# Swapping the two 32-query blocks of the early half in an attention kernel, so that every row tile has five value products

## The reference, cut to what matters

```python
xn = layernorm(x, g_in)                       # x: (64, 128, 512)
q = (xn @ Wq).reshape(b, n, 16, 64).transpose(0, 2, 1, 3) * 64 ** -0.5
k, v = split(xn @ Wkv)                        # one k and one v head of 64, plus a null key and value
sim = einsum('bhid,bjd->bhij', q, k) + bias   # bias: (16, 128, 128), and a null column
sim = where(causal_mask, neg, sim)            # query i sees keys 0..i and the null key
sim = where(mask_p[:, None, None, :], sim, neg)
out = einsum('bhij,bjd->bhid', softmax(sim), v)
return x + layernorm(out.reshape(b, n, 1024) @ Wo, g_out)
```

## Time and profile before

| what | value |
|---|---|
| three timed runs | 1069.54, 1069.09, 1062.03 us (median 1069.09) |
| profiled execution, its own time | 1064.88 us |
| its span, from the first to the last instruction | 1063.0 us |
| mean granted TensorE clock | 0.989 of full speed |

### The profile page before, as it was taken

The page is one execution under the profiler, slowest core; times in us unless marked ns, Lnnn a source line. Parts: engine busy times, 40 slices in busy tenths (PEclk is TensorE's granted clock), DMA queues, the critical chain, the costliest instruction groups (busy, mean ns, idle before and its releaser), DMA issues.

```text
span 1063.0 us, 42980 instructions
## 1 busy us (share of the span) xinstructions
PE 1029.5 (97%) x14254; PEld 902.9 (85%) x14254; DVE 765.8 (72%) x3513; ACT 661.2 (62%) x2620; POOL 828.9 (78%) x1488
## 2 busy tenths in 40 slices
PE   6789999999999999999999999999999999999986
PEld 6678898888888888888888888888888889889875
DVE  4777777777777777786777787776777777777663
ACT  5655675666675665675665676565676565666552
POOL 2867887778878778878778788788788778787775
PEclk8999999999999999999999999999999999999998
DMA  7312222232222222222223122223222223121101
GB/s 213 124 34 86 77 81 89 67 94 76 63 85 82 74 87 73 68 84 85 76 82 91 50 87 84 86 70 89 62 78 85 83 73 93 54 84 59 50 25 60
DMA packets 90013, 84.01 MB, mean 79 GB/s; under 512 B 21568, under 2 KB 64064, under 8 KB 89792
## 3 DMA queue, kind: packets, MB, share of 16 engines
q1 hardware_dynamic: 88336, 81.03, 25.3%
q10 hardware_dynamic: 1456, 0.04, 0.1%
HBM read 40.11 MB, written 16.78 MB: 54 GB/s over the span
## 4 chain that ended last, share of the span: by engine, by line
PE 89%; issue 2%; POOL 2%; ACT 2%; DVE 1%; POOLq 0%; DVEq 0%; ACTq 0%
PE ps_proj L500 38%; PE ps_pv L488 33%; PE ps_s L452 9%; PE ps_pv L477 9%; ACT exp_bot L914 1%; POOL w_nrm L1112 1%; ACT exp_top L914 1%; POOL y_out L1156 0%; POOL y_nrm L1152 0%; DVE logit_bot L608 0%; DVE o_lo L630 0%; POOL bias_b L1103 0%; ACT xn L942 0%; POOL small L1138 0%; DVE wt L624 0%
## 5 line engine op out<-in xcount | busy, mean ns | idle before, releaser
L914 ACT ACTIVATE exp_bot<-logit_bot,neg_max 128x129 f32<-128x129 f32 x512 | 201.6, 399 | 252.0 <-DVE neg_max L608 223.0
L1103 POOL TENSOR_TENSOR bias_b<-bias_c,mask_add 128x256 f32<-128x256 f32 (+1 forms) x512 | 291.9, 599 | 45.3 <-DVE neg_max L608 45.2
L500 PE MATMUL ps_proj<-xt_hi,wq_hi 128*128 128x256 f32 x1024 | 302.5, 295 | 7.5 <-DVE q_sb L690 6.0
L500 PE MATMUL ps_proj<-xt_lo,wq_hi 128*128 128x256 f32 x1024 | 288.6, 282 | 0.9 <-issue 0.9
L500 PE MATMUL ps_proj<-xt_hi,wq_lo 128*128 128x256 f32 x1024 | 288.6, 282 | 0.0
L608 DVE CUSTOM_DVE_ANT_0 logit_bot<-ps_s,bias_b 128x128 f32<-128x128 f32 x512 | 128.3, 288 | 180.1 <-PE ps_s L452 162.4
L500 PEld LDWEIGHTS ps_proj<-xt_hi,wq_hi 128*128 128x128 f32 x1024 | 193.3, 189 | 24.9 <-issue 13.0
L1112 POOL TENSOR_TENSOR w_nrm<-exp_bot,w_inv 128x256 f32<-128x256 f32 x256 | 156.9, 613 | 65.2 <-DVE w_inv L617 65.2
L488 PE MATMUL ps_pv<-wo_hi,o_hi 128*128 128x512 f32 x488 | 199.0, 408 | 1.2 <-DVE o_lo L630 1.2
L488 PE MATMUL ps_pv<-wo_lo,o_hi 128*128 128x512 f32 x488 | 193.5, 397 | 0.0
L500 PEld LDWEIGHTS ps_proj<-xt_hi,wq_lo 128*128 128x128 f32 x1024 | 193.4, 189 | 0.0
(11 more groups left out here) (94 smaller groups left out, 1778.6 us busy)
## 6 DMA issues: line engine op xcount, KB each, us to landing
x_in<-in_x_dram SPq DMA_DIRECT2D x32, 512.0 KB, 4.1
x_res<-in_x_dram SPq DMA_DIRECT2D x64, 256.0 KB, 2.9
out_dram<-y_out SPq DMA_DIRECT2D x64, 256.0 KB, 2.1
x_split<-xn SPq DMA_DIRECT2D x480, 32.0 KB, 1.9
v_rep<-v_raw SPq DMA_DIRECT2D x256, 32.0 KB, 1.9
w_raw<-in_L_cond_Wq_dram SPq DMA_DIRECT2D x4, 512.0 KB, 11.7
w_raw<-in_L_cond_Wo_dram SPq DMA_DIRECT2D x4, 512.0 KB, 5.2
mask_u<-in_mask_BxS_bk_dram SPq DMA_DIRECT2D x31, 32.0 KB, 3.7
```

The costliest lines, as they stand in the source:

```text
L500: mm = pe.matmul(ps[:, 0:TOK], w[:, k, cols], xt[:, slot, k], start=(j == 0), stop=(j == len(todo) - 1))
L914: ins = nc.scalar.activation(out_[:, s, j], in_[:, s, j], ACT.Exp, bias=neg_max[:, s, k:k + 1], scale=-1.0, accum_out=w_sum[:, s, k:k + 1])
L1103: ins = nc.gpsimd.tensor_tensor(out_, bias, key_mask, ALU.add)
```

## The change

x's query and key blocks are put in the order 1, 0, 2, 3 within a batch (`PLACED`): the two 32-token blocks of the early half trade places. The row tile that has three late products then has two early ones (block 1, key blocks 0 and 1), and the one with four late products has one early (block 0). The products per row tile become 5, 5, 5, 5 in place of 4, 6, 4, 6; there are still 40 matmuls in the program per call. What goes with it:

- `split_x` writes to the swapped block, and PE's two early transposes become matmuls with `placing`, a permuted identity, made on DVE at the start.
- Stores and reloads of the residual are three DMAs (32, 32 and 64 rows) in place of one, `PIECES` = 3.
- The mask is added in swapped order by two DVE instructions in place of one.
- The bias is loaded by 12 DMAs into a spare buffer (`q_sb` of the second slot) and made head by head: five GpSimd instructions for each of four, and a `causal_early` mask of its own, built at the start. DVE waits for the bias before it first writes that slot of `q_sb`.

The core of the diff (the semaphore counts that follow from three pieces are left out):

```diff
+PLACED = (1, 0, 2, 3)
 ITEMS = (
-    [(1, 0), (1, 1), (1, 2), (0, 0)],
-    [(1, 0), (1, 1), (1, 2), (1, 3), (0, 0), (0, 1)],
+    [(1, 0), (1, 1), (1, 2), (0, 0), (0, 1)],
+    [(1, 0), (1, 1), (1, 2), (1, 3), (0, 1)],
 )
...
+        placing = sb("placing", [P, P])

...
-        COL_LOADS, ROW_LOADS, BIAS_LOADS, V_LOADS = 4, 2, 8, 8
+        COL_LOADS, ROW_LOADS, BIAS_LOADS, V_LOADS = 4, 2, 12, 8
+        bias_raw = q_sb[:, 1].rearrange("p c u n -> p (c u n)")[:, 0:CB * (BOT + TOP)].rearrange(
+            "p (c n) -> p c n", c=CB)
+        PIECES = 3
         SPLITS = (N // BLK) * (P // BLK)
...
             return o[:, g // 2].rearrange("p c (l h q) -> p c l h q", l=2, h=2)[:, :, :, g % 2]
+
+        def early_swapped(keys_):
+            return keys_.rearrange("p e (a j) -> p e a j", j=BLK)[:, :, 1::-1]
+
+        def placed(rows):
+            return ((rows[0:BLK], slice(BLK, HALF)), (rows[BLK:HALF], slice(0, BLK)), (rows[HALF:N], slice(HALF, N)))
...
             def load_res(q, i):
-                sp.dma_start(x_res[:, i % GB], x_pairs[q, :, i, :]).then_inc(ld_res[i % GB], 16)
+                for rows, at in placed(x_pairs[q, :, i, :]):
+                    sp.dma_start(x_res[at, i % GB], rows).then_inc(ld_res[i % GB], 16)
...
                     for r in range(P // BLK):
-                        sp.dma_start(x_split[BLK * r:BLK * (r + 1), :, a],
+                        sp.dma_start(x_split[BLK * r:BLK * (r + 1), :, PLACED[a]],
                                      xn[BLK * a:BLK * (a + 1), :, P * r:P * (r + 1)]).then_inc(ld_split, 16)
...
                 for e in range(2):
-                    sp.dma_start(bias_c[up, :, N * e:N * (e + 1)], by_head[u, e, HALF:N]).then_inc(ld_bias, 16)
-                    sp.dma_start(bias_c[up, :, BOT + HALF * e:BOT + HALF * (e + 1)],
-                                 by_head[u, e, 0:HALF, :, 0:HALF]).then_inc(ld_bias, 16)
+                    sp.dma_start(bias_raw[up, :, N * e:N * (e + 1)], by_head[u, e, HALF:N]).then_inc(ld_bias, 16)
+                    for a in range(2):
+                        row = HALF * u + BLK * PLACED[a]
+                        sp.dma_start(bias_raw[row:row + BLK, :, BOT + HALF * e:BOT + HALF * (e + 1)],
+                                     by_head[u, e, BLK * a:BLK * (a + 1), :, 0:HALF]).then_inc(ld_bias, 16)
             load_x(0, 1)
...
                         k, b = KX * i + j // GB, j % GB
-                        mm = pe.transpose(ps[:, N * j:N * (j + 1)], xn[:, b, P * k:P * (k + 1)], ident[:])
+                        mm = pe.matmul(ps[:, N * j:N * (j + 1)], xn[:, b, P * k:P * (k + 1)], placing[:],
+                                       start=(j == 0), stop=(j == KX * GB - 1))
                 elif kind == "kv":
...
                 pe.wait_ge(ident_made, 1)
+                pe.wait_ge(placing_made, 2)
                 for _ in range(WARM):
...
                 wait(dve, bias_b_made, CG * (f - 1))
-                nc.vector.tensor_scalar(mask_add[:, k], mask_u8[:, k], MASKED, -MASKED, ALU.mult,
-                                        ALU.add).then_inc(mask_made, 1)
+                nc.vector.tensor_scalar(mask_add[:, k, :, 0:HALF].rearrange("p b (a j) -> p b a j", j=BLK),
+                                        early_swapped(mask_u8[:, k, :, 0:HALF]), MASKED, -MASKED, ALU.mult, ALU.add)
+                nc.vector.tensor_scalar(mask_add[:, k, :, HALF:N], mask_u8[:, k, :, HALF:N], MASKED, -MASKED,
+                                        ALU.mult, ALU.add).then_inc(mask_made, 1)
...
             nc.vector.memset(logit_top[:, :, :, HALF:HALF + 1], 0.0).then_inc(filled, 1)
+            dve.wait_ge(ident_made, 1)
+            nc.vector.tensor_copy(placing[:].rearrange("p (a j) -> p a j", j=BLK)[:, 0:2],
+                                  ident[:].rearrange("p (a j) -> p a j", j=BLK)[:, 1::-1]).then_inc(placing_made, 1)
+            nc.vector.tensor_copy(placing[:, HALF:N], ident[:, HALF:N]).then_inc(placing_made, 1)
             x_stats_of(0, 0)
...
                 inverse(3, 3)
+                dve.wait_ge(bias_made, 3 * CB)
                 q_copies(1, 0)
...
             pool.wait_ge(causal_made, 2)
+            nc.gpsimd.memset(causal_early[:], 0.0).then_inc(early_zero, 1)
+            pool.wait_ge(early_zero, 1)
+            for u in range(2):
+                row = HALF * u + BLK
+                nc.gpsimd.memset(causal_early[row:row + BLK, 0:BLK], -MASKED).then_inc(early_filled, 1)
+            pool.wait_ge(early_filled, 2)
+            for g in range(P // BLK):
+                row, h = BLK * g, g % 2
+                own = causal_early[row:row + BLK, BLK * h:BLK * (h + 1)]
+                nc.gpsimd.affine_select(out=own, in_=own, compare_op=ALU.is_ge, fill=-MASKED, base=0,
+                                        pattern=[[-1, BLK]], channel_multiplier=1).then_inc(early_filled, 1)
+            pool.wait_ge(early_filled, 6)
             pool.wait_ge(filled, 1)
...
-            def make_bias(i):
-                cs = slice(2 * i, 2 * i + 2)
-                for k, part in enumerate((bias_c[:, cs, 0:BOT], bias_c[:, cs, BOT:])):
-                    part = part.rearrange("p c (e n) -> p c e n", e=2)
-                    shift = nb_row[:, cs].unsqueeze(3).to_broadcast(list(part.shape))
-                    nc.gpsimd.tensor_tensor(part, part, shift, ALU.subtract).then_inc(bias_shifted, 1)
-                pool.wait_ge(bias_shifted, 2 * i + 2)
-                for keys_, part in ((N, bias_c[:, cs, 0:BOT]), (HALF, bias_c[:, cs, BOT:])):
-                    own = part.rearrange("p c (e n) -> p c e n", e=2)[:, :, :, keys_ - HALF:keys_]
-                    mask_ = causal[:].unsqueeze(1).unsqueeze(1).to_broadcast(list(own.shape))
-                    nc.gpsimd.tensor_tensor(own, own, mask_, ALU.add).then_inc(bias_made, 1)
-                pool.wait_ge(bias_made, 2 * i + 2)
+            def make_bias(c):
+                null = nb_row[:, c].unsqueeze(2).to_broadcast([P, 2, HALF])
+                null_blocks = nb_row[:, c].unsqueeze(2).unsqueeze(3).to_broadcast([P, 2, 2, BLK])
+                raw_late, raw_early = bot_top(bias_raw[:, c])
+                late, early = bot_top(bias_c[:, c])
+                nc.gpsimd.tensor_tensor(late[:, :, 0:HALF].rearrange("p e (a j) -> p e a j", j=BLK),
+                                        early_swapped(raw_late[:, :, 0:HALF]), null_blocks,
+                                        ALU.subtract).then_inc(bias_made, 1)
+                nc.gpsimd.tensor_tensor(late[:, :, HALF:N], raw_late[:, :, HALF:N], null,
+                                        ALU.subtract).then_inc(bias_shifted, 1)
+                nc.gpsimd.tensor_tensor(early.rearrange("p e (a j) -> p e a j", j=BLK), early_swapped(raw_early),
+                                        null_blocks, ALU.subtract).then_inc(bias_shifted, 1)
+                pool.wait_ge(bias_shifted, 2 * c + 2)
+                for own, mask_ in ((late[:, :, HALF:N], causal), (early, causal_early)):
+                    nc.gpsimd.tensor_tensor(own, own, mask_[:].unsqueeze(1).to_broadcast([P, 2, HALF]),
+                                            ALU.add).then_inc(bias_made, 1)
+                pool.wait_ge(bias_made, 3 * c + 3)
...
                 make_bias(0)
+                make_bias(1)
                 bias(0)
                 bias(1)
-                make_bias(1)
+                make_bias(2)
+                make_bias(3)
                 x_rstd_of(1)
...
```

More of the change, by code:

```diff
@@ L105, in attention_block @@
         causal = sb("causal", [P, HALF])
+        causal_early = sb("causal_early", [P, HALF])
         eps_col = cols(2)
@@ L180, in attention_block @@
         causal_zero, causal_made = sem("causal_zero"), sem("causal_made")
+        early_zero = sem("early_zero")
+        placing_made, early_filled = sem("placing_made"), sem("early_filled")
         filled = sem("filled")
@@ L364, in store @@
                 apart(sp)
-                sp.dma_start(out_pairs[p + back // (2 * GB), :, back % (2 * GB), :], y_out[:, b]).then_inc(stored[b], 16)
+                for rows, at in placed(out_pairs[p + back // (2 * GB), :, back % (2 * GB), :]):
+                    sp.dma_start(rows, y_out[at, b]).then_inc(stored[b], 16)
                 if reload:
@@ L369, in _ @@
             for b in range(GB):
-                sp.sem_inc(stored[b], 16)
+                sp.sem_inc(stored[b], 16 * PIECES)
             load_x(0, 0)
@@ L432, in _ @@
             for b in range(GB):
-                sp.wait_ge(stored[b], 16 * GROUPS + 16)
+                sp.wait_ge(stored[b], 16 * PIECES * (GROUPS + 1))
         @block.tensor
@@ L895, in last_out @@
                 dve.wait_ge(y_rstd_made, B)
-                dve.wait_ge(ld_res[b], 16 * GROUPS)
-                dve.wait_ge(stored[b], 16 * GROUPS)
+                dve.wait_ge(ld_res[b], 16 * PIECES * GROUPS)
+                dve.wait_ge(stored[b], 16 * PIECES * GROUPS)
```

(6 more changed lines are left out.)

## The result

The changed kernel takes 1083.98 us (median of 4 runs, 1083.03 to 1085.23), the kernel before in the same session 1067.82 (4 runs). The ratio is 1.0162 with a 95% interval of 1.012 to 1.0204: slower by some 1.6%, clear of no change, and above the range of the prediction. The profiled execution has a span of 1083.4 us against 1063.0, so 20.4 us have to be found.

A forecast was written before the change was run, and what follows sets the result against it. The prediction took PE, busy without a gap from 110 to 1020 us, as the bound. Its terms, -12.7 + 3.3 + 0 + 0.7 = -8.7 us, gave a forecast of 1057.5 us, range 1049 to 1075.

The forecast's parts named there:

- the waves: PE's value calls: two of 12 matmul waves go, 0.205 us in each of 62 calls, 12.7 us gained.
- The rival that issue holds PE to 17 ns a start: Value calls: issue of the 80 matmuls sets the pace, no waves saved, +4.0 us, 1070 us; chance 0.10.
- the start: Before the loop: longer bias work on GpSimd, later bias DMAs and doubled transposes cost 3.3 us, bounds 1.8 and 7.0.
- what PE saves in this stretch is saved whole: From 110 to 1020 us PE is busy for 908.76 of 910 us, so its savings count fully unless another engine falls behind.
- the loop's other edits: DVE's two-part mask and SP's pieces in the loop: x's load issued 3.8 us later, covered by slack, costing nothing.
- the rival: SP's queue in the loop: pieces cost 0.59 us an issue, x comes late, PE waits, +20 us, 1077 us; chance 0.21.
- The end: Storing the last row by SP after the loop: three issues in place of one cost 0.7 us, bounds 0 and 0.8.

The follow-up runs named there:

- b_even: The kernel before with only the list of value products changed, evened to five per row tile: 1064.87 us, ratio 0.9983.
- b_even_hifirst: The kernel before with even value products and the output projection's eight `o_hi` products put first: 1050.51 us, ratio 0.9859.
- its control: The kernel before with only the output projection's `o_hi` products put first: 1060.75 us, ratio 0.9947.
- a_w14_onepiece: The changed kernel with 14 warming matmuls in place of 30, and x's reload and y's store in one piece each in the loop: 1066.67 us, ratio 1.0007.
- a_warm14: The changed kernel with 14 warming matmuls in place of 30: 1099.06 us, ratio 1.0312.
- a_w14_loads: The changed kernel with 14 warming matmuls in place of 30, and SP's loads of x and mask ahead of the store and reload: 1063.8 us, ratio 0.9985.
- a_warm22: The changed kernel with 22 warming matmuls in place of 30: 1081.03 us (2 runs).
- b_warm46: The kernel before with 46 warming matmuls in place of 30: 1090.16 us, ratio 1.0208.
- a_onepiece: The changed kernel with x's reload and y's store in one piece each in the loop: 1086.18 us, ratio 1.0161.

## Why the prediction was wrong

**Right: the waves.** "A call loses two waves", taken as 0.205 us: 1.64 to 1.43, the 55 calls 86.6 to 74.9 us where no pause stands in them, 0.21 each, 20 in flight to the end. The rival that issue holds PE to 17 ns a start is out.

**Right: the start.** 3.3 us forecast; the first value call starts at 59.14, before at 55.75, +3.4. This is one execution each; the traces of all runs give 54.9 to 57.5 for the five kernels with the old start and 57.2 to 59.1 for the nine with the new, 2.1 us apart in the mean. The parts were less exact than their sum: the bias came 0.5 us sooner (22.77 against 23.27) where 0.5 later was forecast, and from there to the scale GpSimd took 2.3 us longer where 1.7 was. GpSimd's twenty bias instructions take 9.5 us (9.1 forecast), and its scale of the second group's x comes at 35.24, 1.8 us later than at 33.40 (2.2 forecast):

```profile
22.77 0.40 POOL L1219 TENSOR_TENSOR bias_c<-q_sb,nb_row 128x128 f32<-128x128 f32 x1 [13.90 <-DMA q_sb<-in_fside_16xSxS_dram]
...
35.24 0.19 POOL L1147 TENSOR_TENSOR small<-x_mv,small 128x2 f32<-128x2 f32 x1
```

**Wrong: "what PE saves in this stretch is saved whole".** This is the first step that failed. Its condition, "as long as no other engine falls behind", was looked into by busy shares and for x alone; I read "busy without a gap" as "PE alone sets the pace". But two chains can end at the same moment, and then the trace shows no wait on either side. ACT's `o_hi` and DVE's `o_lo` ended just as PE came to the projection: +7.6 and +1.3 us in the table. In half of the calls ACT begins `o_hi` only when its exponentials of the scores ahead are done, 1.74 us after the call's start, with the change or without; in the other half `o_hi` did come sooner, by 0.09 us of the 0.21 (1.73 to 1.64), and why not by all of it stays open. `b_even` shows it by itself: 11.6 us saved in the value calls, 13.0 lost ahead of the projection, some 4 of them by the recurring pause; `b_even_hifirst` against its control gives the saving back. What would have told it beforehand is the distance from the last `o_lo` that the projection's start needs to its first matmul, call by call: 0.053 to 0.055 us in 48 of 55 calls, too even for anything but a wait. I had looked at the slack of x, and not at that of the chain that consumes the very result that comes sooner.

**Wrong: "the loop's other edits: nothing".** The mechanism was right and a size off: that of the pair of store and reload, whose four more issues were taken at +1.9 us, at 0.36 an issue and 0.12 of gap. From the first store to the issue behind the reload, the pair ahead of x's load takes 4.83 us in place of 1.35 (medians of 27 each), the pair ahead of the spread of v 3.61 in place of 1.28 (30 each): +3.5 and +2.3, together 5.8 where 3.8 was counted. Most of it is the issues themselves: they take 3.46 us in place of 0.71 in the first pair and 2.59 in place of 0.78 in the second, so 0.57 us for each of the eight added issues, and 0.15 for each added gap. That is the price of the rival (0.59 and 0.13, 6.4 us for both pairs) and not the 0.36 to which I leaned. A piece of 32 rows is issued in 0.36 us (store) and 0.44 (reload), one of 64 rows in 0.56 and 0.55 (medians), a whole one in 0.36 and 0.35; and in the pair ahead of x's load 24 of the 162 issues take over 1 us, before none:

```profile
L350 SPq DMA_DIRECT2D x_res<-in_x_dram x192: 331/442/1403, 31.7 to 1071.5; - x192
...
L381 SPq DMA_DIRECT2D out_dram<-y_out x192: 320/365/1526, 86.6 to 1080.7; - x192
```

The load did land sooner after its issue, as forecast (median 3.7 against 4.1), which did not suffice. In the changed kernel this costs 6.7 us; without the pauses it is 32.7 (316.8 against 284.1), more than the rival's +20. The rival's mechanism, DVE waiting for x_in and PE for q_sb behind it, is what the traces show; its 1077 us was short because it kept the gain of the waves and knew nothing of the pause, and that it came as near as it did is chance, since x cost 6.7 us there and not 20. The Trainium skill, "DMA: Bandwidth & Descriptors", section "Rules for kernel authors", advises one transfer over all 128 partitions in place of two over halves of them, since both would use the same DMA engines. The advice holds where the pieces stand ahead of x's load, with -32.4 us for one piece (`a_w14_onepiece` against `a_warm14`); its reason no run here shows, as the loss is SP's issue time ahead of that load (`a_w14_loads` keeps the three pieces and is as fast).

**Missing: the code's place.** This is the largest loss. PE's transposes were counted at their time in the start, +1.1 us. That 16 pairs more ahead of the loop shift everything behind them stood nowhere, and the pauses take 14.0 us of the loop. That the place decides is shown: 16 pairs more in the kernel before bring the pause, 16 fewer in the changed kernel take it out of the call, 8 fewer move it by 8. What PE waits for there is argued, not shown. The trace has a queue of instructions, with as many packets in both kernels (page, part 3, after):

```profile
q8 instruction: 138, 2.26, 0.9%
```

That is 16 KB a packet, and each of the 13 pauses of the changed kernel and of `a_warm22` ends 2.3 to 3.0 us after such a packet has started. In `b_warm46` and `a_onepiece`, whose pauses last up to 2.1 us, each ends 2.2 to 2.5 us after one; there the packet starts 0.25 and 0.29 us behind the start of the value call (medians of 13), in the changed kernel 0.55 us ahead of it. So a pause is long where its packet starts late; what moves the packet stays open. The kernel before has a packet at this point of every pass too, and its place lies just 16 matmuls further on: 69 + 16 = 85, the 80 of the call and five of the projections, where `b_even` shows it.

The Trainium skill, "Advanced Engine Details and Errata", section "ISA Cache", states lines of 16 KB, which hold 256 instructions; the packets' size agrees. A score step and a value call have 112 pairs, 224 instructions, which go out in 0.83 + 1.36 = 2.2 us: about the time from a packet's start to PE's resuming. On this reading PE uses up code here about as fast as it arrives, and stands where a packet's border falls in this stretch; in the projections, at 0.12 us a pair, it would stand less, as it does in the kernel before. That PE waits for its code is thus the likely cause, but no run held the packets back or sent them sooner.

**The end** was forecast at +0.7 and came to nothing that one trace can tell: the time from the sixtieth value call to the end is 68.3 us, before 68.5, with five value calls in it.

The sum, then: -8.7 forecast for the whole program. In the measured loop -11.7 for the calls, and +14.0 for the pause, +7.6 and +1.3 for the projection, +6.7 for x: +17.9; with the start and the end +20.4.

## What to carry to other kernels

An engine that is busy without a gap can still be one of two chains that end together. Before counting a saving, take the consumer of the result that comes sooner and measure how long its other inputs have been ready: with no slack there, the saving goes into a wait, and the cheap cure is to let the consumer start on what it already has (with the eight `o_hi` products first the even products were worth 10.2 us in place of 1.2). Such a wait shows even where no idle time does: the consumer starts at the same distance behind its input in call after call.

Losses do not add: a pause on the busiest engine can hide a late transfer, and taking one loss away can make the time worse (+15 us for the removal of the pause). Take them away in pairs before acquitting any.

Where a loop sends out many small matmuls, its time can hang on how many instructions stand ahead of it. Change that number by itself once, before a difference is put down to the edit.

## What the runs showed of the hardware

The place of code ahead of a loop was worth 23 us here: `b_warm46` differs from the kernel before by 16 matmuls, and takes 1090.16 us against 1067.23; its first value call starts no later (54.92 against 55.75). Its pauses last up to 2.1 us and come once in each pass.

Each of the 65 pauses inside value calls (13 in each of the five kernels that have them) ended 2.2 to 3.0 us after a 16 KB packet of the instruction queue had started.

DMAs of 32 or 64 of 128 rows are not cheaper to issue than whole ones: 435 and 549 ns for the pieces of x_res (medians) against 349 for the whole, before any gap.
